# A decoder layer on one core: the second slice of the experts' down product as three split products, and the halves of the up split exchanged between VectorE and GpSimd

## The chip, the core and the metric

The kernel runs on one core of a Trainium2 chip. The metric is the device time of one execution in microseconds (us). The kernel before the change took 1047.9 us (median of three runs, 1045.63 to 1049.46).

## What is computed

One decoder layer for 896 tokens (8 sequences of 112) of width 512, all in float32: self-attention with 16 heads and a window mask, cross-attention with 16 heads of 128 over 375 context rows, and a feed-forward layer of one shared expert (hidden width 704, which the kernel takes as two units of 352) and 8 routed experts (hidden width 352), two of them per token. A layer norm follows each. The change touches only the routed experts:

```python
for e in range(N_EXPERTS):
    we = jnp.sum(jnp.where(topk_idx == e, w, 0.0), axis=-1)
    gu = xf @ up_w[e].T
    g_e, u_e = jnp.split(gu, 2, axis=-1)
    h = jax.nn.silu(g_e) * u_e
    out = out + h @ down_w[e].T * we[:, None]
```

## The kernel before

**Precision.** TensorE's products are taken in one of two ways. Most go through `three_products` (L84 to L88): both operands are split into a high part in the type fp32r and a low part, the rest, and high x high, low x high and high x low are added in one PSUM bank. A few are plain float32 matmuls. Making a split costs a cast on ScalarE (high) and a subtraction on VectorE or GpSimd (low = raw - high).

**Sorted blocks.** The tokens' rows are scattered to a buffer in HBM (`sorted_x`), sorted by expert, in NB = 21 blocks of 128 rows; each block belongs to one expert and has its own load of that expert's weights. Unit u = j + 1 serves block j; unit 22 (LAST_U) is the second half of the shared expert. A unit is 4 chunks of up weights (each 128 x 704) and 3 slices of down weights (each 128 x 512; the third has 96 rows that count). The raw weights and the low up parts lie in rings of three buffers (`raw`, `low`), the high up parts in two (`high`).

**One block step j**, the unit in which this text counts:

- TensorE (L2305 to L2313): `block_up(j)` (24 matmuls of 352 columns), `turn_block(j + 1)` (4 transposes, the next block's rows), `block_down(j - 1)`, `turn_hidden(j)` (3 transposes of the hidden block). `block_up` waits for the split rows `xb_lo` and both halves of its unit's low up parts; `turn_hidden` waits for `mul_done`, the hidden block.
- ScalarE (L1535 to L1543): `up_high(j + 2)` casts four chunks, then silu, `block_x(j + 1)` (high part of the next rows), `hidden_out(j)` (copies the turned hidden block out of PSUM), `third_high(j)` (cast of the third down slice).
- VectorE (L1895 to L1908): `up_low(j + 2)` subtracts chunks 0 and 1, then the product that makes `h_blk` (L1899, sets `mul_done`), `block_low(j + 1)` (`xb_lo`), `take(j - 1)` (a down result out of PSUM), `hidden_third_low(j)`, `third_low(j)`.
- GpSimd (L1320 to L1326): chunks 2 and 3 of the same `up_low`, and nothing else in this stage.
- The SP queue starts the loads and stores of every block.

All these are instruction streams written out by hand; each engine runs its own in order, and semaphores join them. The order on an engine is thus the order of the lines. `block_down` before the change (L2204 to L2217) takes slices 1 and 2 of the hidden width as float32 matmuls on `hT` and the raw weights, and slice 3 by `three_products`:

```python
for c in range(2):
    w = slice(DC * CHUNK + c * D, DC * CHUNK + (c + 1) * D)
    pe.matmul(ey_ps[:, n % 2, :], hT[:, c * P:(c + 1) * P], raw[u % RING][:, w], start=(c == 0), stop=False)
```

**After the blocks** comes the last unit: six steps k of `dense_up`, whose VectorE part (L1910 to L1918) also adds the gathered expert rows to the result (`combine`, three per step) and splits the last down weights (`down_low`, at k == 4), then the down products and the last layer norm.

Of the kernel before, what the change touches and what calls it, by code (L numbers as in the profile page):

```python
# [185 lines left out]
def expert_views(nc):  # L186

    F, E, NB = F32, EXPERTS, SLOT_TILES
    pad = 2 * 2 * TOK + 2 * HT + 2 * 2 * KVP + 2 * KT_N * PW - 2 * HC * TOK - 4 * HT
    front = [("h_hi", [HC, TOK], F32R), ("h_lo", [HC, TOK], F32R), ("silu_g", [2, HT], F), ("h_full", [2, HT], F), ("pad", [pad], F),  # L190
             ("y_sb", [2, D], F), ("gate_w", [DC, E], F), ("gate_b", [E], F), ("gate_hl", [DC, 2, E], F32R),
             ("before", [P], F32R), ("every", [P], F32R), ("iota_e", [TILES, E], F), ("level", [E, TILES], F), ("upto", [E, E], F),
             ("iota_j", [NB, E], F)]
    blocks = [("x_nat", [2, D], F), ("xb_hi", [D], F32R), ("xb_lo", [D], F32R),
              ("h_blk", [HPAD], F), ("hT", [2 * P], F), ("h3_hi", [P], F32R), ("h3_lo", [P], F32R), ("logitsT", [TOK], F), ("score", [TILES, E], F), ("chosen", [TILES, E], F),
              ("onehot", [2, TILES, E], F), ("weighed", [2, TILES, E], F), ("picked", [TILES, E], F32R), ("slot_of", [TILES, E], F),
              ("top_v", [TILES, 8], F), ("top_i", [TILES, 8], U32), ("top_f", [TILES, 8], F), ("top_w", [2, TILES], F),
              ("total", [2, TILES], F), ("mix", [2, TILES], F), ("over", [E, TILES], F), ("run", [E, E], F), ("n_tiles", [E], F),
              ("ends", [E], F), ("starts", [E], F), ("passed", [NB, E], F), ("owner_f", [NB], F), ("owner", [NB], U32),
              ("slots_f", [2 * TILES], F), ("slots", [2 * TILES], U32)]  # L200
# [734 lines left out]
def cross_and_experts(nc, env, w_pairs, ctx_nat, ctx_split, gateT, gate_bias, w_units, sorted_x, sorted_y, out, ended):  # L935
# [11 lines left out]
    with ExitStack() as es:  # L947
# [3 lines left out]
        def ps(name, shape):  # L951
# [15 lines left out]
        n_tiles, ends, starts, passed = v["n_tiles"], v["ends"], v["starts"], v["passed"]  # L967
        owner_f, owner, slots_f, slots = v["owner_f"], v["owner"], v["slots_f"], v["slots"]
        gu_ps, et_ps, ey_ps = v["gu_ps"], v["et_ps"], v["ey_ps"]
        h3_hi, h3_lo = v["h3_hi"], v["h3_lo"]  # L970
        THIRD = slice(UNIT_W - D, UNIT_W)
        rest = HID - 2 * P
        first_down_ps = [ey_ps[:, 0], ey_ps[:, 1], gu_ps[:, 0, 0], gu_ps[:, 0, 1], gu_ps[:, 1, 0], gu_ps[:, 1, 1], ey_ps[:, 0]]

# [35 lines left out]
        names_x = """gate_loaded consts_set more_consts gate_hi_done gate_lo_done logitsT_ready logitsT_copied logits_ready logits_added  # L1010
            logits_exp router places_ready owner_ready slots_ready cleared xb_turned xb_hi_done xb_lo_done
            up_ready silu_done mul_done h_hi_done h_lo_done h_turned
            hT_done h3_hi_done h3_lo_done third_hi_done third_lo_done y_ready y_taken y_stored combined stored""".split()
        names_x += [f"{part}_{k}_loaded" for part in ("up", "down") for k in range(1, RING)]
        names_x += [f"x_{k}_loaded" for k in range(2)] + [f"y_{k}_stored" for k in range(2)]
        names_x += [f"scattered_{t}" for t in range(TILES)]
# [217 lines left out]
        def _(pool):  # L1234
# [84 lines left out]

            def up_low(u):  # L1320

                for c in (2, 3):
                    cols = slice(c * CHUNK, (c + 1) * CHUNK)
                    pool.wait_ge(xs["up_hi_done"], DC * u + c + 1)
                    pool.tensor_tensor(low[u % RING][:, cols], raw[u % RING][:, cols], high[u % 2][:, c, :].bitcast(F32),
                                       ALU.subtract).then_inc(xs["up_lo_g"], 1)  # L1326
# [38 lines left out]
        def _(act):  # L1365
# [96 lines left out]
            def third_high(j):  # L1462
# [3 lines left out]
                act.wait_ge(xs["y_ready"], TILES + max(j - 1, 0))  # L1466
                act.copy(down_hi[0:rest, j % 2 * D:(j % 2 + 1) * D], raw[u % RING][0:rest, THIRD]).then_inc(xs["third_hi_done"], 1)

            def hidden_out(j):

                act.wait_ge(xs["h_turned"], j + 1)
                act.copy(hT[:], et_ps[:, 1, 0:2 * P]).then_inc(xs["hT_done"], 1)
                act.copy(h3_hi[0:rest], et_ps[0:rest, 1, 2 * P:3 * P]).then_inc(xs["h3_hi_done"], 1)

            def block_x(j):
                act.wait_ge(xs["xb_turned"], j + 1)
# [76 lines left out]
        def _(dve):  # L1553
# [232 lines left out]
            def third_low(j):  # L1786
# [4 lines left out]
                dve.tensor_tensor(down_lo[0:rest, j % 2 * D:(j % 2 + 1) * D], raw[u % RING][0:rest, THIRD], part.bitcast(F32),  # L1791
                                  ALU.subtract).then_inc(xs["third_lo_done"], 1)

            def hidden_third_low(j):

                dve.wait_ge(xs["h3_hi_done"], j + 1)
                dve.tensor_tensor(h3_lo[0:rest], et_ps[0:rest, 1, 2 * P:3 * P], h3_hi[0:rest].bitcast(F32),
                                  ALU.subtract).then_inc(xs["h3_lo_done"], 1)

            def combine(n):  # L1800

# [87 lines left out]
            for t in range(TILES - 1):  # L1889
                add_shared(t, 0)  # L1890
                if t in (2, 4):
                    up_low(1, t // 2 - 1)
                if t == TILES - 3:
                    block_low(0)
            for j in range(NB):  # L1895
# [10 lines left out]
                    take(j - 1)  # L1906
                hidden_third_low(j)
                third_low(j)  # L1908
            take(NB - 1)
            gated(0, UPS + NB)  # L1910
            for k in range(1, UPS):
                gated(k, UPS + NB)
                hidden_low(1, k - 1)
                if k == 4:
                    down_low(1, LAST_U)
                for n in range(3 * k - 3, min(3 * k, GATHERS)):
                    combine(n)
# [10 lines left out]
        def _(pe):  # L1928
# [265 lines left out]
            def turn_hidden(j):  # L2194

                pe.wait_ge(xs["mul_done"], UPS + j + 1)
                if j >= 1:
                    pe.wait_ge(xs["hT_done"], j)
                    pe.wait_ge(xs["h3_lo_done"], j)
                for c in range(HC):  # L2200
                    mm = pe.transpose(et_ps[:, 1, c * P:(c + 1) * P], h_blk[:, c * P:(c + 1) * P], ident[:])
                mm.then_inc(xs["h_turned"], 1)
# [1 line left out]
            def block_down(j):  # L2204
# [2 lines left out]
                pe.wait_ge(xs["hT_done"], j + 1)  # L2207
                pe.wait_ge(xs[f"down_{u % RING}_loaded"], 16 * (u // RING + 1))
                pe.wait_ge(xs["y_taken"], n - 1)
                for c in range(2):  # L2210
                    w = slice(DC * CHUNK + c * D, DC * CHUNK + (c + 1) * D)
                    pe.matmul(ey_ps[:, n % 2, :], hT[:, c * P:(c + 1) * P], raw[u % RING][:, w], start=(c == 0), stop=False)  # L2212
                pe.wait_ge(xs["h3_lo_done"], j + 1)
                pe.wait_ge(xs["third_lo_done"], j + 1)
                third = slice(j % 2 * D, (j % 2 + 1) * D)
                three_products(pe, ey_ps[:, n % 2, :], h3_hi[0:rest], h3_lo[0:rest], down_hi[0:rest, third], down_lo[0:rest, third],
                               False, True).then_inc(xs["y_ready"], 1)  # L2217

            def output(t, bank):

# [194 lines left out]
```

## Time and profile before

| what | value |
|---|---|
| three runs, median | 1047.9 us (1045.63, 1047.9, 1049.46) |
| the profiled execution, its own time | 1046.03 us |
| its span, first to last instruction | 1044.3 us |
| granted TensorE clock, mean | 0.999 of full speed |
| busy share of the span: TensorE / VectorE / ScalarE / GpSimd | 98% / 69% / 51% / 51% |
| the block stage | about 844 to 991 us, 21 steps of some 7.0 us |
| the last unit and the end | about 991 to 1044 us |

The busy share of an engine is the part of the span in which one of its instructions was being worked on. It is a mean over stages with different limits, so the text below reads the block stage by itself. The three runs differ by 0.37%.

### The profile page before, as it was taken

To read this page: it belongs to the slowest core of one execution; us is meant where nothing else is said; L and a number is where in the kernel's file an instruction comes from. 1 tells how busy PE (TensorE), PEld (TensorE's weight loads), DVE (VectorE), ACT (ScalarE), POOL (GpSimd) and SP (SyncE) were. 2 spreads that over 40 slices of the span, in tenths; PEclk is the share of its full clock that TensorE was granted. 3 is DMA by queue.
4 is the path that set the end of the run, shared out by engine and by line. 5 is a ranking of instruction groups with operands and counts; after the bars stand their busy time and mean duration, and the time that the engine had idled before them with its cause. 6 is when DMAs were issued, how large, how long until landed. Compare 5 with 4: busy or idle time off the path is not lost.

```text
span 1044.3 us, 20310 instructions
## 1 busy us (share of the span) xinstructions
PE 1018.9 (98%) x7021; PEld 910.0 (87%) x7021; DVE 722.6 (69%) x1496; ACT 536.6 (51%) x1075; POOL 532.7 (51%) x515
## 2 busy tenths in 40 slices
PE   8999999999999999999999999999999999999997
PEld 8856678999999999999999999999987888888885
DVE  4268876776767767767776776766886476666648
ACT  5355555555545455455555554554553356676610
POOL 1257767745534634643634634634474545544544
PEclk9999999999999999999999999999999999999999
DMA  8100114324333233323223233234220779999843
GB/s 279 83 32 2 61 39 153 143 109 157 116 108 114 99 107 111 101 109 116 96 111 115 94 117 109 98 118 136 98 90 1 286 282 386 387 393 399 294 119 113
DMA packets 45273, 153.46 MB, mean 147 GB/s; under 512 B 3768, under 2 KB 4792, under 8 KB 42144
## 3 DMA queue, kind: packets, MB, share of 16 engines
q1 hardware_dynamic: 42976, 145.38, 38.6%
q0 software_dynamic: 2240, 7.34, 2.1%
q8 instruction: 34, 0.56, 0.2%
q14 instruction: 23, 0.19, 0.0%
HBM read 130.04 MB, written 22.66 MB: 146 GB/s over the span
## 4 chain that ended last, share of the span: by engine, by line
PE 72%; POOL 5%; DVE 4%; issue 3%; ACT 1%; DMA 1%; POOLq 0%; DVEq 0%; ACTq 0%
PE xa_y_ps L86 6%; PE xa_y_ps L88 5%; PE xa_y_ps L87 5%; PE ex_raw_gu_ps L86 4%; PE ex_raw_gu_ps L88 4%; PE ex_raw_gu_ps L87 4%; PE xa_c_ps L1990 4%; PE xa_c_ps L1986 4%; PE xa_c_ps L1985 3%; PE ex_raw_ey_ps L2212 3%; PE xa_turn_ps L2067 3%; PE xa_turn_ps L2023 3%; PE front_k_ps L86 3%; PE front_k_ps L88 3%; PE front_k_ps L87 3%
## 5 line engine op out<-in xcount | busy, mean ns | idle before, releaser
L1300 POOL TENSOR_TENSOR xa_probs<-xa_probs,xa_inv_sum 112x750 f32<-112x750 f32 x63 | 97.9, 1553 | 75.5 <-DVE xa_inv_sum L1640 75.5
L1589 DVE TENSOR_TENSOR xa_kT_lo<-xa_turn_ps,xa_kT_hi 128x750 fp32r<-128x750 f32 x63 | 59.2, 939 | 99.9 <-ACT xa_kT_hi L1388 99.8
L1285 POOL TENSOR_TENSOR k_ms<-k_ss,sum_eps 125x6 f32<-125x6 f32 x63 | 12.6, 200 | 210.8 <-DVE k_ss L1605 210.8
L1985 PE MATMUL xa_c_ps<-xa_probsT_hi,xa_nat 125*128 125x224 f32 x384 | 92.3, 274 | 2.7 <-ACT xa_probsT_hi L1404 2.7
L1986 PE MATMUL xa_c_ps<-xa_probsT_hi,xa_nat 125*128 125x224 f32 x384 | 92.3, 275 | 0.0
L1404 ACT CAST xa_probsT_hi<-xa_turn_ps 125x672 fp32r<-125x672 f32 x62 | 44.6, 720 | 87.2 <-PE xa_turn_ps L2067 87.2
L1288 POOL TENSOR_TENSOR k_inv<-k_ms,neg_half 125x6 f32<-125x6 f32 x63 | 83.5, 1325 | 8.3 <-POOL k_ms L1285 6.7
L1410 ACT ACTIVATE xa_probs<-xa_scores_ps,xa_bias,xa_q_scale 112x375 f32<-112x375 f32 x126 | 82.8, 663 | 5.9 <-DVE xa_bias L1615 4.7
L1985 PEld LDWEIGHTS xa_c_ps<-xa_probsT_hi,xa_nat 125*128 125x128 f32 x384 | 73.6, 192 | 3.5 <-issue 3.1
L1986 PEld LDWEIGHTS xa_c_ps<-xa_probsT_hi,xa_nat 125*128 125x128 f32 x384 | 73.5, 191 | 0.5
L86 PE MATMUL front_k_ps<-land_xa_wk_hi,land_xa_ctx 128*125 128x256 f32 x252 | 71.4, 283 | 1.6 <-DVE front_k_hat L1632 1.2
L87 PE MATMUL front_k_ps<-land_xa_wk_hi,land_xa_ctx 128*125 128x256 f32 x252 | 70.8, 281 | 0.0
L88 PE MATMUL front_k_ps<-land_xa_wk_lo,land_xa_ctx 128*125 128x256 f32 x252 | 70.8, 281 | 0.0
L1384 ACT ACTIVATE front_k_sq<-front_k_ps 125x512 f32<-125x512 f32 x63 | 37.7, 598 | 62.0 <-PE front_k_ps L88 60.4
L1990 PE MATMUL xa_c_ps<-xa_probsT_lo,xa_nat 125*128 125x224 f32 x384 | 64.0, 275 | 0.8 <-DVE xa_probsT_lo L1621 0.8
L1584 DVE TENSOR_TENSOR xa_cT_lo<-xa_c_ps,xa_cT_hi 128x448 fp32r<-128x448 f32 x61 | 38.0, 622 | 37.9 <-ACT xa_cT_hi L1379 37.9
L1605 DVE TENSOR_REDUCE k_ss<-front_k_sq 125x6 f32<-125x768 f32 x63 | 59.7, 948 | 5.7 <-ACT front_k_sq L1392 5.7
L423 POOL TENSOR_TENSOR sa_masked<-sa_masked,sa_row_max 112x448 f32<-112x448 f32 x32 | 30.3, 947 | 60.5 <-DVE sa_row_max L653 60.0
L1392 ACT ACTIVATE front_k_sq<-xa_k_ps 125x256 f32<-125x256 f32 x63 | 24.3, 386 | 70.7 <-PE xa_k_ps L88 70.7
L1379 ACT CAST xa_cT_hi<-xa_c_ps 128x448 fp32r<-128x448 f32 x61 | 32.6, 535 | 52.4 <-PE xa_c_ps L1990 52.4
L1611 DVE TENSOR_REDUCE xa_row_max<-xa_scores_ps 112x2 f32<-112x750 f32 x63 | 58.4, 928 | 0.0
L1621 DVE TENSOR_TENSOR xa_probsT_lo<-xa_turn_ps,xa_probsT_hi 125x672 fp32r<-125x672 f32 x62 | 53.1, 856 | 5.3 <-ACT xa_probsT_hi L1404 4.7
(423 smaller groups left out, 3545.0 us busy)
## 6 DMA issues: line engine op xcount, KB each, us to landing
xa_nat<-ctx_split SPq DMA_DIRECT2D x56, 750.0 KB
ex_raw_raw<-in_w_units SPq DMA_DIRECT2D x15, 1408.0 KB, 8.2
ex_raw_raw<-in_w_units SPq DMA_DIRECT2D x15, 768.0 KB
land_ex_raw<-in_w_units SPq DMA_DIRECT2D x8, 1408.0 KB, 8.3
land_ex_raw<-in_w_units SPq DMA_DIRECT2D x8, 768.0 KB, 8.0
ctx_split<-xa_nat SPq DMA_DIRECT2D x8, 750.0 KB
sorted_x<-ex_raw_y_sb SPq DMA_DIRECT2D x7, 768.0 KB, 10.6
ex_raw_x_nat<-sorted_x SPq DMA_DIRECT2D x21, 256.0 KB, 8.6
```

The lines of the kernel that those rows point to most:

```text
L86: pe.matmul(out, st_hi, mv_hi, start=first, stop=False)
L87: pe.matmul(out, st_lo, mv_hi, start=False, stop=False)
L88: return pe.matmul(out, st_hi, mv_lo, start=False, stop=last)
L1288: pool.tensor_tensor(k_inv[0:KT, :], k_ms[0:KT, :], env["neg_half"][0:KT, 0:2 * KT_N], ALU.pow).then_inc(sem["kinv_done"], 1)
L1300: pool.tensor_tensor(probs[0:T, u % 2], probs[0:T, u % 2], inv_sum[0:T, u % 2, :].unsqueeze(2).broadcast_to([T, 2, KV]), ALU.mult).then_in ...
L1410: act.activation(probs[0:T, u % 2, h, :], scores_ps[0:T, h, 0:KV], ACT.Exp, bias=bias[0:T, u % 2, h:h + 1], scale=q_scale[0:T, u % B // HA ...
L1589: dve.tensor_tensor(kT_lo[:, :, 0:KV], turn_ps[:, :, 0:KV], kT_hi[:, :, 0:KV].bitcast(F32), ALU.subtract).then_inc(sem["kT_lo_done"], 1)
L1605: dve.tensor_reduce(k_ss[0:KT, :], k_sq[0:KT, :].rearrange("p (a d) -> p a d", d=XA_DH), AX_X, ALU.add).then_inc(sem["kss_done"], 1)
L1611: dve.tensor_reduce(row_max[0:T, u % 2, :], scores_ps[0:T, :, 0:KV], AX_X, ALU.max).then_inc(sem["max_done"], 1)
L1985: pe.matmul(c_view[:, c], nat[0:KT, u % 2, 0, at], probsT_hi[0:KT, :, cols], start=(t == 0), stop=False)
L1986: pe.matmul(c_view[:, c], nat[0:KT, u % 2, 1, at], probsT_hi[0:KT, :, cols], start=False, stop=False)
L1990: mm = pe.matmul(c_view[:, c], nat[0:KT, u % 2, 0, at], probsT_lo[0:KT, :, cols], start=False, stop=(t == KT_N - 1))
```

## The change

Three edits. (1) In `block_down` the second slice of the hidden width goes through `three_products`, after the third; for it ScalarE casts 256 columns of the turned hidden block to fp32r, copies 128 and casts a second down slice (`second_high`), and VectorE subtracts 256 columns and that slice (`second_low`). (2) In `up_low` GpSimd now takes chunks 0 and 1 and VectorE chunks 2 and 3; this holds for units 1 to 22 (unit 0 is split elsewhere). (3) In the last unit `down_low` moves from k == 4 to k == 3.

```diff
@@ gpsimd, up_low @@
-    for c in (2, 3):
+    for c in (0, 1):
@@ scalar @@
+def second_high(j):
+    u = j + 1
+    act.wait_ge(xs["y_ready"], TILES + j)
+    act.copy(second_hi, raw[u % RING][:, SECOND]).then_inc(xs["second_hi_done"], 1)
...
 def hidden_out(j):
     act.wait_ge(xs["h_turned"], j + 1)
-    act.copy(hT[:], et_ps[:, 1, 0:2 * P]).then_inc(xs["hT_done"], 1)
-    act.copy(h3_hi[0:rest], et_ps[0:rest, 1, 2 * P:3 * P]).then_inc(xs["h3_hi_done"], 1)
+    act.copy(h23_hi[:], et_ps[:, 1, P:3 * P]).then_inc(xs["h23_hi_done"], 1)
+    act.copy(hT[:], et_ps[:, 1, 0:P]).then_inc(xs["hT_done"], 1)
...
     hidden_out(j)
     third_high(j)
+    second_high(j)
@@ vector, up_low @@
-    for c in chunks or (0, 1):
+    for c in chunks or (2, 3):
...
+def second_low(j):
+    u = j + 1
+    dve.wait_ge(xs["second_hi_done"], j + 1)
+    dve.tensor_tensor(second_lo, raw[u % RING][:, SECOND], second_hi.bitcast(F32),
+                      ALU.subtract).then_inc(xs["second_lo_done"], 1)
...
 def hidden_third_low(j):
-    dve.wait_ge(xs["h3_hi_done"], j + 1)
-    dve.tensor_tensor(h3_lo[0:rest], et_ps[0:rest, 1, 2 * P:3 * P], h3_hi[0:rest].bitcast(F32),
-                      ALU.subtract).then_inc(xs["h3_lo_done"], 1)
+    dve.wait_ge(xs["hT_done"], j + 1)
+    dve.tensor_tensor(h23_lo[:], et_ps[:, 1, P:3 * P], h23_hi[:].bitcast(F32),
+                      ALU.subtract).then_inc(xs["h23_lo_done"], 1)
...
     hidden_third_low(j)
     third_low(j)
+    second_low(j)
...
-    if k == 4:
+    if k == 3:
         down_low(1, LAST_U)
@@ tensor, block_down @@
-    for c in range(2):
-        w = slice(DC * CHUNK + c * D, DC * CHUNK + (c + 1) * D)
-        pe.matmul(ey_ps[:, n % 2, :], hT[:, c * P:(c + 1) * P], raw[u % RING][:, w], start=(c == 0), stop=False)
-    pe.wait_ge(xs["h3_lo_done"], j + 1)
+    bank = ey_ps[:, n % 2, :]
+    pe.matmul(bank, hT[:], raw[u % RING][:, DC * CHUNK:DC * CHUNK + D], start=True, stop=False)
+    pe.wait_ge(xs["h23_lo_done"], j + 1)
     pe.wait_ge(xs["third_lo_done"], j + 1)
     third = slice(j % 2 * D, (j % 2 + 1) * D)
-    three_products(pe, ey_ps[:, n % 2, :], h3_hi[0:rest], h3_lo[0:rest], down_hi[0:rest, third], down_lo[0:rest, third],
-                   False, True).then_inc(xs["y_ready"], 1)
+    three_products(pe, bank, h23_hi[0:rest, P:2 * P], h23_lo[0:rest, P:2 * P], down_hi[0:rest, third], down_lo[0:rest, third],
+                   False, False)
+    pe.wait_ge(xs["second_lo_done"], j + 1)
+    three_products(pe, bank, h23_hi[:, 0:P], h23_lo[:, 0:P], second_hi, second_lo, False, True).then_inc(xs["y_ready"], 1)
```

What stands in a row on the engines that matter. In these rows the lines of the changed kernel are its own, and the tile names are those of the buffers as the program first gave them (`ex_raw_h_hi` is `h3_hi` or `h23_hi`, `land_ex_down_hi` holds the high down slices, `ex_low_low` and `land_low_low` are buffers of `low`).

VectorE, one block step, before:

```order
L1791 TENSOR_TENSOR land_ex_down_lo<-ex_raw_raw,land_ex_down_hi 96x512
L1667 TENSOR_TENSOR ex_low_low<-ex_raw_raw,land_ex_up_hi 128x704 x2
L1899 TENSOR_TENSOR ex_raw_h_blk<-ex_raw_silu_g,ex_raw_gu_ps 128x352
L1675 TENSOR_TENSOR ex_raw_xb_lo<-ex_raw_et_ps,ex_raw_xb_hi 128x512
L1784 COPY ex_raw_y_sb<-ex_raw_ey_ps 128x512
L1797 TENSOR_TENSOR ex_raw_h_lo<-ex_raw_et_ps,ex_raw_h_hi 96x128
```

and the same step after the change:

```order
L1799 TENSOR_TENSOR land_ex_down_lo<-ex_raw_raw,land_ex_down_hi 96x512
L1806 TENSOR_TENSOR land_ex_down_lo<-ex_raw_raw,land_ex_down_hi 128x512
L1675 TENSOR_TENSOR ex_low_low<-ex_raw_raw,land_ex_up_hi 128x704 x2
L1914 TENSOR_TENSOR ex_raw_h_blk<-ex_raw_silu_g,ex_raw_gu_ps 128x352
L1683 TENSOR_TENSOR ex_raw_xb_lo<-ex_raw_et_ps,ex_raw_xb_hi 128x512
L1792 COPY ex_raw_y_sb<-ex_raw_ey_ps 128x512
L1812 TENSOR_TENSOR ex_raw_h_lo<-ex_raw_et_ps,ex_raw_h_hi 128x256
```

One subtraction (L1806) is new, one is wider (L1812), and the pair of low up parts, still ahead of the product that makes `h_blk`, is now that of chunks 2 and 3.

ScalarE, one block step after the change; before, L1474 was not there, the first cast had 96 x 128 and the copy, ahead of it, 128 x 256:

```order
L1479 CAST ex_raw_h_hi<-ex_raw_et_ps 128x256
L1480 COPY ex_raw_hT<-ex_raw_et_ps 128x128
L1468 CAST land_ex_down_hi<-ex_raw_raw 96x512
L1474 CAST land_ex_down_hi<-ex_raw_raw 128x512
L1437 CAST land_ex_up_hi<-ex_raw_raw 128x704 x4
L1546 ACTIVATE ex_raw_silu_g<-ex_raw_gu_ps 128x352
L1486 CAST ex_raw_xb_hi<-ex_raw_et_ps 128x512
```

The four casts of the up chunks and everything behind them stand one 128 x 512 cast later.

## Rows read from the trace of the kernel before

**Rows 1.** Windows of two block steps: busy us of each engine, clock, DMA share
```profile
core 0: us, PE busy (x) PEld busy (x) DVE busy (x) ACT busy (x) POOL busy (x), PEclk, DMA share, GB/s
893.80:900.80 7.00, 7.00 (x39) 5.82 (x38) 4.55 (x8) 4.78 (x10) 3.48 (x2) 1.00 1.02 386
900.80:907.80 7.00, 7.00 (x40) 5.85 (x39) 4.51 (x8) 4.75 (x10) 3.48 (x2) 1.00 1.01 405
```
**Rows 2.** Chain that ended last, one block step: start us, us, what
```profile
899.98 0.21 PE ex_raw_gu_ps L86
...
903.86 0.44 PE ex_raw_et_ps L2173 x4
904.29 1.72 PE ex_raw_ey_ps L2212 x4
906.01 0.23 PE ex_raw_ey_ps L86
906.24 0.23 PE ex_raw_ey_ps L87
906.47 0.23 PE ex_raw_ey_ps L88
906.70 0.33 PE ex_raw_et_ps L2201 x3
907.03 0.18 PE ex_raw_gu_ps L86
```
**Rows 3.** Timeline of ScalarE, the same step: start us, us, instruction [idle before]
```profile
900.02 0.37 ACT L1472 COPY ex_raw_hT<-ex_raw_et_ps 128x256 f32<-128x256 f32 x1 [2.17 <-PE ex_raw_et_ps L2201]
900.29 0.26 ACT L1473 CAST ex_raw_h_hi<-ex_raw_et_ps 96x128 fp32r<-96x128 f32 x1
900.45 0.62 ACT L1467 CAST land_ex_down_hi<-ex_raw_raw 96x512 fp32r<-96x512 f32 x1
900.97 2.83 ACT L1436 CAST land_ex_up_hi<-ex_raw_raw 128x704 fp32r<-128x704 f32 x4
903.89 0.46 ACT L1539 ACTIVATE ex_raw_silu_g<-ex_raw_gu_ps 128x352 f32<-128x352 f32 x1
904.33 0.59 ACT L1479 CAST ex_raw_xb_hi<-ex_raw_et_ps 128x512 fp32r<-128x512 f32 x1
```
**Rows 4.** Timeline of VectorE, the same step
```profile
901.10 0.69 DVE L1791 TENSOR_TENSOR land_ex_down_lo<-ex_raw_raw,land_ex_down_hi 96x512 fp32r<-96x512 f32 x1 [0.23 <-ACT land_ex_down_hi L1467]
901.78 1.69 DVE L1667 TENSOR_TENSOR ex_low_low<-ex_raw_raw,land_ex_up_hi 128x704 fp32r<-128x704 f32 x2
904.39 0.52 DVE L1899 TENSOR_TENSOR ex_raw_h_blk<-ex_raw_silu_g,ex_raw_gu_ps 128x352 f32<-128x352 f32 x1 [0.91 <-ACT ex_raw_silu_g L1539]
904.95 0.69 DVE L1675 TENSOR_TENSOR ex_raw_xb_lo<-ex_raw_et_ps,ex_raw_xb_hi 128x512 fp32r<-128x512 f32 x1
```
**Rows 5.** Timeline of GpSimd, the same step
```profile
903.19 3.48 POOL L1325 TENSOR_TENSOR ex_low_low<-ex_raw_raw,land_ex_up_hi 128x704 fp32r<-128x704 f32 x2 [3.54 <-ACT land_ex_up_hi L1436]
```
**Rows 6.** Timeline of VectorE and GpSimd in the first block step
```profile
844.45 0.88 DVE L1667 TENSOR_TENSOR ex_low_low<-ex_raw_raw,land_ex_up_hi 128x704 fp32r<-128x704 f32 x1
845.25 2.40 DVE L1667 TENSOR_TENSOR ex_low_low<-ex_raw_raw,land_ex_up_hi 128x704 fp32r<-128x704 f32 x1
844.45 2.45 POOL L1325 TENSOR_TENSOR ex_low_low<-ex_raw_raw,land_ex_up_hi 128x704 fp32r<-128x704 f32 x1 [4.92 <-ACT land_ex_up_hi L1436]
846.86 2.36 POOL L1325 TENSOR_TENSOR ex_low_low<-ex_raw_raw,land_ex_up_hi 128x704 fp32r<-128x704 f32 x1
```
**Rows 7.** Timeline of VectorE and GpSimd in the cross-attention
```profile
666.05 1.44 POOL L1300 TENSOR_TENSOR xa_probs<-xa_probs,xa_inv_sum 112x750 f32<-112x750 f32 x1 [1.44 <-DVE xa_inv_sum L1640]
667.45 1.18 POOL L1242 TENSOR_TENSOR xa_q_ms<-xa_q_ss,sum_eps 112x4 f32<-112x4 f32 x1
666.41 2.16 DVE L1053 TENSOR_TENSOR xa_wo_lo<-xa_wo_raw,xa_wo_hi 128x1024 fp32r<-128x1024 f32 x1
```
**Rows 8.** Line L1053: count, duration ns min/median/max, first and last start
```profile
L1053 DVE TENSOR_TENSOR xa_wo_lo<-xa_wo_raw,xa_wo_hi x8: 1330/2159/2165, 188.5 to 746.0; 128x1024 fp32r<-128x1024 f32 x8
```
**Rows 9.** Line L1899, the same columns
```profile
L1899 DVE TENSOR_TENSOR ex_raw_h_blk<-ex_raw_silu_g,ex_raw_gu_ps x21: 520/521/522, 848.4 to 988.9; 128x352 f32<-128x352 f32 x21
```
**Rows 10.** Timeline of VectorE in the last unit
```profile
1015.08 1.63 DVE L1807 SCALAR_TENSOR_TENSOR resid<-ex_raw_raw,ex_raw_mix,resid 128x512 f32<-128x512 f32 x2
1017.08 0.76 DVE L1807 SCALAR_TENSOR_TENSOR resid<-ex_raw_raw,ex_raw_mix,resid 128x512 f32<-128x512 f32 x1 [0.37 <-DMA ex_raw_raw<-sorted_y,ex_raw_slots]
1018.90 0.62 DVE L1753 TENSOR_TENSOR ex_raw_h_full<-ex_raw_silu_g,ex_raw_gu_ps 128x448 f32<-128x448 f32 x1 [1.07 <-issue]
1020.04 1.75 DVE L1679 TENSOR_TENSOR land_ex_down_lo<-ex_raw_raw,land_ex_down_hi 128x1536 fp32r<-128x1536 f32 x1
```

More of the change, by code:

```diff
@@ L194, in expert_views @@
     blocks = [("x_nat", [2, D], F), ("xb_hi", [D], F32R), ("xb_lo", [D], F32R),
-              ("h_blk", [HPAD], F), ("hT", [2 * P], F), ("h3_hi", [P], F32R), ("h3_lo", [P], F32R), ("logitsT", [TOK], F), ("score", [TILES, E], F), ("chosen", [TILES, E], F),
+              ("h_blk", [HPAD], F), ("hT", [P], F), ("h23_hi", [2 * P], F32R), ("h23_lo", [2 * P], F32R), ("logitsT", [TOK], F), ("score", [TILES, E], F), ("chosen", [TILES, E], F),
               ("onehot", [2, TILES, E], F), ("weighed", [2, TILES, E], F), ("picked", [TILES, E], F32R), ("slot_of", [TILES, E], F),
@@ L969, in cross_and_experts @@
         gu_ps, et_ps, ey_ps = v["gu_ps"], v["et_ps"], v["ey_ps"]
-        h3_hi, h3_lo = v["h3_hi"], v["h3_lo"]
-        THIRD = slice(UNIT_W - D, UNIT_W)
+        h23_hi, h23_lo = v["h23_hi"], v["h23_lo"]
+        SECOND, THIRD = slice(UNIT_W - 2 * D, UNIT_W - D), slice(UNIT_W - D, UNIT_W)
+        second_hi, second_lo = down_hi[:, 2 * D:3 * D], down_lo[:, 2 * D:3 * D]
         rest = HID - 2 * P
@@ L1012, in cross_and_experts @@
             up_ready silu_done mul_done h_hi_done h_lo_done h_turned
-            hT_done h3_hi_done h3_lo_done third_hi_done third_lo_done y_ready y_taken y_stored combined stored""".split()
+            hT_done h23_hi_done h23_lo_done second_hi_done second_lo_done third_hi_done third_lo_done y_ready y_taken y_stored combined stored""".split()
         names_x += [f"{part}_{k}_loaded" for part in ("up", "down") for k in range(1, RING)]
@@ L1891, in _ @@
                 if t in (2, 4):
-                    up_low(1, t // 2 - 1)
+                    up_low(1, t // 2 + 1)
                 if t == TILES - 3:
@@ L2198, in turn_hidden @@
                     pe.wait_ge(xs["hT_done"], j)
-                    pe.wait_ge(xs["h3_lo_done"], j)
+                    pe.wait_ge(xs["h23_lo_done"], j)
                 for c in range(HC):
```

## The prediction

> **What bounds the kernel now.** I read the table of busy shares first and then only the block stage, where all but one small edit lies. The windows of two block steps [rows 1] show TensorE busy for 7.00 of 7.00 us at a clock of 1.00, ScalarE 4.8, VectorE 4.5, GpSimd 3.5. The chain of waits [rows 2] runs through TensorE alone: 24 up matmuls from 899.98, four transposes at 903.86, two float32 down products (four pieces, 1.72), three split products of 0.23, three transposes, and the next step at 907.03. So a step is 7.05 us of TensorE work. DMA is full as well (share 1.01 to 1.02, 386 to 405 GB/s), yet nothing on TensorE waits for it.
>
> The other engines are to be read by when they end. I count from H, the end of `turn_hidden(j)` (899.98 in the rows). ScalarE starts at H+0.04, its four up casts begin at H+0.99 and end at H+3.82, and silu starts at H+3.91, 0.03 after TensorE's last up matmul [rows 3]: no slack ahead of silu. VectorE makes its two low up parts from H+1.80 to 3.49 and then waits for silu [rows 4]. GpSimd starts on its parts at H+3.21 and ends at H+6.69 [rows 5], 0.36 before TensorE wants them. Thus VectorE's pair and GpSimd's pair hardly overlap in time.
>
> **Part 1: the product itself.** Removed per block: one float32 product, 1.72/2 = 0.86. Added: three at 0.23 = 0.70 [rows 2]. TensorE's work falls by 0.16, to 6.89 a step; over 21 blocks 3.4 us, if TensorE stays the bound.
>
> The Trainium skill (FP8 and Floating Point Precision, TensorE Precision Notes) says that a true float32 product makes four passes through the array. Three passes against four would save a quarter of 0.86, 0.215 a block and 4.5 us in all, as an estimate. The rows have 0.23 for each split product rather than 0.215, and I go by the rows.
>
> **Part 2: ScalarE.** The cast of 256 columns and the copy of 128 have the column counts of the two rows before, in the other order, and cost the same 0.43 until the next start. New is `second_high`, 512 columns: from the third slice's cast to the next start is 0.52 [rows 3]. Its own start waits for nothing new: the down product that frees its buffer ends before H. So the up casts start at H+1.51, 0.52 later. Each takes 0.68 to the next and 0.78 in all ((2.83-0.78)/3), so they end at H+2.29, 2.97, 3.66, 4.34. Silu starts at about 4.27 and ends at 4.73, 0.36 later than before. TensorE wants the hidden block at 6.56 (4.31, the end of the transposes, plus 0.86 + 1.40 for the down product, with 0.01 of rounding): alone, this is hidden.
>
> **Part 3: VectorE and GpSimd.** `hidden_third_low` grows from 128 to 256 columns, by some 0.13; it ends before `third_low` can start, at H+1.13. `second_low` adds one 0.69 subtraction, from about 1.81 to 2.50. GpSimd now may start once the first up cast is done, at 2.29 + 0.08 = 2.37. VectorE's pair needs the third and the fourth cast and can't start before 3.70. So the exchange, which starts GpSimd earlier, puts the two pairs on top of each other.
>
> What that costs is in two other stages. In the first block step both engines started a low part at 844.45 [rows 6]. VectorE's first took its usual 0.88; GpSimd's took 2.45 instead of some 1.7; VectorE's second took 2.40 instead of 0.88; GpSimd's second 2.36. In the cross-attention [rows 7] VectorE issued a 1024-column subtraction of two SBUF operands at 666.41 while GpSimd's multiply ran to 667.49. It took 2.16, against 1.33 for the shortest of the eight [rows 8], and ended 1.08 after that multiply: beside it, it can't have done more than a small part of its work. GpSimd's next instruction, on four columns, then took 1.18. One engine stands still until the other's whole instruction is done. The product that makes `h_blk`, with one operand in PSUM, took 520 to 522 ns in all 21 steps [rows 9], though in steps like this one GpSimd was at work beside it [rows 5].
>
> The Trainium skill (SBUF — State Buffer, Who interferes with whom) states the same as a rule against this change: a VectorE instruction with two SBUF inputs and a GpSimd instruction that reads SBUF hold a shared port in turn, each for its whole length. The traces agree.
>
> Now one step. A GpSimd part holds the port for some 1.6 and a VectorE part for 0.75 (846.86 to 847.65 in [rows 6], less the wait). GpSimd's first part asks at 2.37, waits for `second_low` until about 2.47 and ends at 4.1. VectorE's chunk 2, asking since 3.70, runs to 4.85. GpSimd's second part, asking since 4.1, runs to 6.45. VectorE's chunk 3 runs to 7.2. The turns alternate, as in [rows 6]. Queued behind chunk 3 on VectorE is the product for `h_blk`: 7.2 + 0.52 = 7.72. TensorE's `turn_hidden` waits for it until 7.78, where it was free at 6.56, and ends at 8.11. `xb_lo` follows at 7.71 to 8.40, so the next `block_up` starts 0.34 after the new H; the next step absorbs this, since its down product ends at H+6.9, ahead of 7.78. A step is thus 8.11 instead of 7.05: +1.06.
>
> It holds in steps 1 to 20. In step 0 the pairs collide before the change too [rows 6], silu ends later than they do, and no `second_high` stands ahead, so nothing changes there: 20 x 1.06 = 21.2 us.
>
> The bounds: if GpSimd keeps the port for both its parts, VectorE ends at about 7.4 and a step is 8.3 (+25 us). If GpSimd's first part doesn't lose 0.1 to `second_low`, a step is 8.0 (+19).
>
> **Part 4: `down_low` a step sooner.** It takes 1.75 and now runs at about 1015.1 to 1016.8, ahead of three `combine` steps, which end by about 1019.1 instead of 1017.8. VectorE was idle for 1.07 before 1018.9 [rows 10], so this fills the gap and at most 0.2 moves on. At its old place 1.75 fall away, behind which VectorE soon waits for silu again. I take 0; it may give 0.1.
>
> **Sum**, against the profiled execution's own 1046.0: +21.2 in the blocks, -0.2 for the last block's down product, which is on TensorE's path, 0 at the end: **1067 us**. The median of the runs is 1.9 above the profiled one; I leave the number and let the range carry it.
>
> **The rivals.** (A) *VectorE gets the port for both its chunks in a row, before GpSimd's second part.* This is the case on the other side. Its place is 4.85 in the step: if chunk 3, ready since 4.34, goes next, VectorE ends at 5.6 and `h_blk` at 6.2, before TensorE wants it. GpSimd then ends at 7.2, and `block_up` waits 0.35 in every second step: a mean of 7.07, 1046 us, no change. It decides at the point where VectorE's pair ends before about 6.0. Against it: in [rows 6] GpSimd cut in after one VectorE part. Chance 0.08. (B) *No blocking in this stage.* Then the pairs end at 5.3 and 5.7, all hidden, and Part 1 comes through: 1042.6, if DMA, already full [rows 1], can give 2% more. Against it stand [rows 6 to 8]. Chance 0.06. (C) *The two engines share instead of taking turns.* In [rows 6] VectorE did 1.69 of work in 3.20. At that rate, from 3.70 on, its pair ends at 6.9 and a step is 7.8: +15, 1061 us. For it: the sums in [rows 6] fit as well. Against it: the times in [rows 7]. Chance 0.13. (D) *Worse still*: TensorE, idle for 1.2 of 8.1 us, is granted less clock, or blocks lose more than I count. The clock reads 1.00 in both windows, but they have no idle time. Above 1075 us, chance 0.03.
>
> **Numbers.** Main case 0.70. The range holds the main case with its bounds (1065 to 1071), up to 2 us for the median's distance, and most of C: 1056 to 1074. A change of 0.5% (5.2 us) is about what can be told from none. Slower: main, C and D, 0.86. Same: A and nearly all of B (3.4 us is 0.33%), 0.12. Faster, which asks for half as much again as B gives: 0.02.
>
> **What would show it.** Right: windows of block steps with TensorE idle for some 1.1 us in each, that idle put down to VectorE's `h_blk`; block steps 8.1 long; low parts on VectorE recorded at well over 0.88 (2.0 and more for chunk 3), on GpSimd over 1.7; DMA share near 0.87. Wrong: VectorE's low parts at 0.88 in all steps (then B), both ending by H+5.7 with GpSimd's second part over 3 us long (then A), or a wait that ends with a cast of ScalarE or a DMA.

## The result and the profile after

The changed kernel takes **1072.27 us** (median of four runs, 1068.14 to 1072.81), the kernel before 1048.08 (four runs, 1045.63 to 1049.46): a ratio of 1.0223, interval 1.0195 to 1.0250. The forecast was 1067, range 1056 to 1074, slower with a chance of 0.86. The profiled execution took 1068.14 (span 1066.4, mean clock 0.999), 22.1 above the profiled one of before; the sum had said 21.0.

The page's first part for the kernel after: busy time, share of the span, instructions.

```profile
PE 1023.4 (96%) x7042; PEld 912.0 (86%) x7042; DVE 768.3 (72%) x1517; ACT 545.3 (51%) x1096; POOL 543.4 (51%) x515
```

TensorE reads as 96% busy, which hides what happened. ScalarE reads the turned hidden block once per block, first by L1472 (a copy) before and by L1479 (a cast) after. Between the first and the last of these 21 instructions lay 140.5 us before, 7.03 a step, and 163.5 after, 8.18 a step. These 20 steps took 23.0 us more, and the rest of the program 0.9 less. Two block steps of after in windows, same columns as [rows 1]:

```profile
899.53:907.70 8.17, 7.30 (x39) 5.99 (x39) 6.80 (x9) 5.18 (x10) 4.02 (x2) 1.00 0.94 338
907.70:915.90 8.20, 7.30 (x39) 5.99 (x39) 6.83 (x9) 5.18 (x10) 4.02 (x2) 1.00 0.94 322
```

TensorE is busy for 7.30 of 8.17 and of 8.20 us where it had no idle time before. VectorE went from 4.5 to 6.8 busy and GpSimd from 3.48 to 4.02, though GpSimd still makes two subtractions of the same size. The clock stays at 1.00.

The chain of waits of after, one step (start us, us, what), to be held against [rows 2]:

```profile
908.79 0.52 ACT land_ex_down_hi L1474
909.31 2.05 ACT land_ex_up_hi L1437 x3
911.36 0.02 issue
911.38 1.60 DVE ex_low_low L1675 x2
912.99 1.77 issue
914.76 0.52 DVE ex_raw_h_blk L1914
915.28 0.04 issue
915.32 0.56 PE ex_raw_et_ps L2217 x3
```

Before, this chain ran through TensorE alone. Now it goes through ScalarE's casts, then `up_low`, then `h_blk`, and TensorE has only its three transposes on it. The 1.77 called "issue" is time in which VectorE stands inside its pair and no record says why.

The timelines of VectorE and of GpSimd in that step (start us, us, instruction, idle before), against [rows 4, 5]:

```profile
909.43 0.68 DVE L1806 TENSOR_TENSOR land_ex_down_lo<-ex_raw_raw,land_ex_down_hi 128x512 fp32r<-128x512 f32 x1
911.38 3.45 DVE L1675 TENSOR_TENSOR ex_low_low<-ex_raw_raw,land_ex_up_hi 128x704 fp32r<-128x704 f32 x2 [1.27 <-ACT land_ex_up_hi L1437]
914.76 0.51 DVE L1914 TENSOR_TENSOR ex_raw_h_blk<-ex_raw_silu_g,ex_raw_gu_ps 128x352 f32<-128x352 f32 x1
915.19 0.68 DVE L1683 TENSOR_TENSOR ex_raw_xb_lo<-ex_raw_et_ps,ex_raw_xb_hi 128x512 fp32r<-128x512 f32 x1
```

GpSimd in the same view:

```profile
910.07 4.02 POOL L1326 TENSOR_TENSOR ex_low_low<-ex_raw_raw,land_ex_up_hi 128x704 fp32r<-128x704 f32 x2 [4.15 <-ACT land_ex_up_hi L1437]
```

VectorE's pair takes 3.45 for what took 1.69, and GpSimd's, from 910.07 to 914.09, runs beside it for 2.7 us. The subtractions have the same 128 x 704 as before. In numbers from H = 907.71: GpSimd asks at 2.36 (forecast 2.37) and ends at 6.38 (6.45). VectorE's pair starts at 3.67 (3.70) and ends at 7.12 (7.2). TensorE's down product ends at 6.85 (6.9), and `turn_hidden` starts at 7.61 (7.78) and ends at 8.17 (8.11).

The waits on TensorE in the block stage of after (us in total, times, longest us):

```profile
PEld ex_raw_et_ps L2217 <- DVE ex_raw_h_blk L1914: 24.5, 20, 1.6
...
PE ex_raw_et_ps L2217 <- DVE ex_raw_h_blk L1914: 15.8, 20, 1.2
```

Twenty times, once for each step 1 to 20, the hidden block is late. No wait of this size on a cast or a DMA stands beside it.

### The profile page after: what moved, and what is told of

Read it like the earlier page. It is cut to its first block, busy times and chain, and to the rows that moved or that the text cites. A ratio compares the mean times of both kernels' runs of the same rounds, so it can differ in the third digit from the quotient of the medians.

```text
span 1066.4 us, 20394 instructions
## 1 busy us (share of the span) xinstructions
PE 1023.4 (96%) x7042; PEld 912.0 (86%) x7042; DVE 768.3 (72%) x1517; ACT 545.3 (51%) x1096; POOL 543.4 (51%) x515
## 4 chain that ended last, share of the span: by engine, by line
PE 60%; ACT 8%; DVE 7%; issue 6%; POOL 4%; POOLq 0%; ACTq 0%; DVEq 0%
PE xa_y_ps L86 6%; PE xa_y_ps L88 5%; PE xa_y_ps L87 5%; PE xa_c_ps L2006 4%; PE xa_c_ps L2002 3%; PE xa_c_ps L2001 3%; PE xa_turn_ps L2083 3%; PE xa_turn_ps L2039 3%; PE front_k_ps L86 3%; PE front_k_ps L88 3%; PE front_k_ps L87 3%; PE ex_raw_gu_ps L86 2%; PE ex_raw_gu_ps L87 2%; PE ex_raw_gu_ps L88 2%; PE xa_scores_ps L2069 2%
```

## The experiments

My theory: a VectorE subtraction with two SBUF operands and a GpSimd subtraction that reads SBUF use one port in turns, each for its whole length. The exchange puts the pairs on top of each other, and `h_blk`, queued behind VectorE's pair, carries the delay to TensorE. Rivals: ScalarE's new cast or VectorE's new subtraction is what makes `h_blk` late, with nothing to do with GpSimd; the two engines' writes collide as well as their reads; the second product itself costs more than it saves. Ratios are to the kernel before on the same chip with their 95% interval. "A step" is the stretch between the first and the last time that ScalarE first reads the turned hidden block, divided by 20, in the run's profile. In the edits, `...` stands for further lines of the same kind (names, and the counts that TensorE waits for).

**1. The change without the exchange.**

```diff
@@ GpSimd, up_low
-                for c in (0, 1):
+                for c in (2, 3):
@@ VectorE, up_low
-                for c in chunks or (2, 3):
+                for c in chunks or (0, 1):
@@ VectorE, the first unit's parts
-                    up_low(1, t // 2 + 1)
+                    up_low(1, t // 2 - 1)
```

> The changed kernel with the exchange alone undone: GpSimd again takes chunks 2 and 3, VectorE 0 and 1; the second product as three split products and the earlier down_low stay. Turn-taking at the port (my theory): VectorE's pair is over by H+3.9, GpSimd's runs from about H+3.9 to H+7.2, TensorE waits some 0.3 us for it in part of the steps: a step of 7.05 to 7.15 us, ratio to before 0.998 to 1.003. Rival, the added ScalarE cast and VectorE subtraction are what costs: all of them are still there, so the time stays near 1.02. Rival, sharing instead of turns: like my theory here, within 1.00.

Measured: 1049.40 us, ratio 1.0020 (1.0007 to 1.0033); a step 7.22, a little above the 7.05 to 7.15 expected. Nearly all of the loss is gone. ScalarE's extra cast and VectorE's extra subtraction are both still there, so neither makes it by itself. From the timelines of VectorE and GpSimd in this run:

```profile
910.66 1.69 DVE L1675 TENSOR_TENSOR ex_low_low<-ex_raw_raw,land_ex_up_lo 128x704 fp32r<-128x704 f32 x2
...
912.06 3.49 POOL L1326 TENSOR_TENSOR ex_low_low<-ex_raw_raw,land_ex_up_lo 128x704 fp32r<-128x704 f32 x2 [4.13 <-ACT land_ex_up_lo L1437]
```

Both pairs have their old lengths. But without the exchange the second product gives nothing either: the casts are later, so GpSimd's pair ends later, and `block_up` now waits for it in half the steps (waits of the block stage; us, times, longest):

```profile
PE ex_raw_gu_ps L86 <- POOL ex_low_low L1326: 3.1, 6, 0.5
...
PE ex_raw_gu_ps L86 <- POOL land_low_low L1326: 2.0, 4, 0.5
```

**2. The exchange alone, on the kernel before** (experiment 1's lines the other way round).

> The kernel before with the exchange alone: GpSimd chunks 0 and 1, VectorE 2 and 3; no second split product. Turn-taking: GpSimd asks at H+1.86, VectorE's first part at H+3.2, the four parts end at about H+6.6 on VectorE, the hidden block at H+7.1: a step of 7.6 to 7.8 us, +11 to +15 us, ratio 1.011 to 1.014. VectorE's parts are recorded at about 1.1 and 2.4 us. Sharing in proportion: VectorE's pair takes 3.2 from H+3.2, a step of about 7.35, ratio 1.006. Rival, the added work costs and not the exchange: ratio 1.000.

Measured: 1062.63 us, 1.0144 (1.0124 to 1.0165); a step 7.63, against 7.03 before and 8.18 after. VectorE's pair, in the timeline of this run, is as long as in the change:

```profile
913.64 3.45 DVE L1667 TENSOR_TENSOR ex_low_low<-ex_raw_raw,land_ex_up_hi 128x704 fp32r<-128x704 f32 x2 [1.36 <-ACT land_ex_up_hi L1436]
```

So the exchange is enough to lose. It loses 12.1 us in the 20 steps and not 23 because the casts come 0.52 earlier without `second_high`: 8.18 less 7.63 is 0.55. In the change, the new cast pushes an already late chain further; in experiment 1 the second product with the same cast costs 0.2 a step in all. The profiled execution of this run took 1067.79 us, the other four 1061.57 to 1063.32. The extra time of the profile lies outside the 20 steps, and most of it ahead of them: ScalarE's first read of the turned hidden block comes at 857.1, where it came at 850.7 before. The last section shows what stood in the way there.

**3. GpSimd's subtraction replaced by two memsets**, which write as many columns and read nothing. Left out: the low weights of chunks 0 and 1, which are zeros here.

```diff
-                    pool.tensor_tensor(low[u % RING][:, cols], raw[u % RING][:, cols], high[u % 2][:, c, :].bitcast(F32),
-                                       ALU.subtract).then_inc(xs["up_lo_g"], 1)
+                    pool.memset(low[u % RING][:, cols].bitcast(F32), 0.0).then_inc(xs["written"], 1)
+                    pool.wait_ge(xs["written"], 2 * (u - 1) + c + 1)
+                    pool.memset(low[u % RING][:, cols].bitcast(F32), 0.0).then_inc(xs["up_lo_g"], 1)
...
```

> The changed kernel, but GpSimd's two low parts are left out: in place of each subtraction it writes zeros over the same 704 columns twice, so it works beside VectorE's pair without reading SBUF. If what VectorE waits for is GpSimd's reading: VectorE's parts are back at 0.88 us each, the pair ends by H+5.3, a step is 6.85 to 6.95, ratio 0.995 to 1.000. If any GpSimd instruction that touches SBUF holds VectorE up: its parts are recorded at over 1 us, for each write of some 0.7 us one wait, the pair ends at H+6 or later, a step is 7.1 or more, ratio 1.00 to 1.01. If the added ScalarE and VectorE work is what costs: 1.02, as the changed kernel.

Measured: 1041.21 us, 0.9957 (0.9941 to 0.9972); a step 6.82, just below the 6.85 to 6.95 expected. The timelines of VectorE and GpSimd show them at work together with no delay:

```profile
908.65 1.69 DVE L1676 TENSOR_TENSOR ex_low_low<-ex_raw_raw,land_ex_up_lo 128x704 fp32r<-128x704 f32 x2 [1.27 <-ACT land_ex_up_lo L1438]
...
908.68 0.69 POOL L1326 MEMSET ex_low_low<- 128x704 f32 x1
909.42 0.69 POOL L1328 MEMSET ex_low_low<- 128x704 f32 x1
```

It isn't GpSimd's being at work, nor its writes; it is its reading beside VectorE's two SBUF operands. The Trainium skill (SBUF — State Buffer, Who interferes with whom) states that a VectorE instruction with two SBUF inputs contends with a GpSimd instruction that reads SBUF, and not with one that only writes it. This run agrees: 1.69 for VectorE's pair beside the memsets, as in experiment 1. That the port is taken for a whole instruction isn't tested here; experiment 7 shows it. The step of 6.82 is also what TensorE needs with the second product split and nothing in its way.

**4. All four low parts on VectorE.**

```diff
@@ GpSimd, up_low
-                for c in (0, 1):
+                for c in ():
@@ VectorE, up_low
-                for c in chunks or (2, 3):
+                for c in chunks or (0, 1, 2, 3):
@@ VectorE, the first unit's parts
-                    up_low(1, t // 2 + 1)
+                    up_low(1, *((0,) if t == 2 else (1, 2, 3)))
...
```

> The changed kernel with all four low parts on VectorE, none on GpSimd. Turn-taking: no one to wait for at the port; four parts back to back from H+2.35 to H+5.55, the hidden block at H+6.0, xb_lo at H+6.6, a step of 6.9 to 7.0, ratio 0.996 to 1.000. So twice the work on VectorE is over sooner than half of it beside GpSimd. Rival, VectorE's load or its place in the chain is what costs: 1.03 or more. Sharing: as turn-taking.

Measured: 1044.49 us, 0.9970 (0.9960 to 0.9980); a step 6.92. VectorE's timeline:

```profile
910.29 3.29 DVE L1675 TENSOR_TENSOR ex_low_low<-ex_raw_raw,land_ex_up_lo 128x704 fp32r<-128x704 f32 x4
```

Four parts in 3.29, where two beside GpSimd took 3.45. In the change, GpSimd's help cost VectorE more than doing the work itself. This also ends the rival that VectorE has too much to do.

**5. The last part behind the hidden block.** VectorE makes chunk 2 where it did, and chunk 3 only after `h_blk` and `xb_lo`. The pairs overlap as before; only what queues behind them changes.

```diff
-                up_low(j + 2)
+                up_low(j + 2, 2)
@@ after block_low(j + 1)
+                up_low(j + 2, 3)
```

> The changed kernel with one line moved on VectorE: chunk 3's low part goes behind the hidden block and xb_lo, chunk 2 stays ahead of them. The port sees the same four parts in the same turns, but the hidden block no longer queues behind the last. Turn-taking with the queue behind it as the price: the hidden block at H+5.3, TensorE's turn_hidden waits for nothing, chunk 3 ends at about H+7.2, which block_up of the next step waits for by 0.3 us in part of the steps: a step of 7.05 to 7.2, ratio 0.999 to 1.004. If the port's turns cost by themselves, wherever they stand in the queue: 1.02 as before the move.

Measured: 1049.77 us, 1.0039 (1.0024 to 1.0054); a step 7.23, just above the 7.05 to 7.2 expected. GpSimd's pair still takes 4.03, but VectorE's two parts are 1.17 and 0.94 (timeline of VectorE):

```profile
904.70 1.17 DVE L1675 TENSOR_TENSOR ex_low_low<-ex_raw_raw,land_ex_up_hi 128x704 fp32r<-128x704 f32 x1 [1.27 <-ACT land_ex_up_hi L1437]
906.06 0.52 DVE L1914 TENSOR_TENSOR ex_raw_h_blk<-ex_raw_silu_g,ex_raw_gu_ps 128x352 f32<-128x352 f32 x1 [0.19 <-ACT ex_raw_silu_g L1546]
...
907.22 0.94 DVE L1675 TENSOR_TENSOR ex_low_low<-ex_raw_raw,land_ex_up_hi 128x704 fp32r<-128x704 f32 x1
```

`h_blk`, which has an operand in PSUM, takes its usual 0.52 while GpSimd's pair (903.39 to 907.42) is under way, and the loss falls from 24 us (2.2%) to 4 (0.4%). What is left of it shows in the waits of the block stage: `block_up` waits for chunk 3's low part 10 times, for up to 0.5 us and 4.6 in all. What cost the time is not the turn itself but who stands behind it in VectorE's queue.

**6. Three parts on VectorE, the last one on GpSimd.** If the theory holds, the product's gain can be had: VectorE takes the chunks as they come, GpSimd only chunk 3, whose read falls at the end of VectorE's three.

```diff
@@ GpSimd, up_low
-                for c in (0, 1):
+                for c in (3,):
@@ VectorE, up_low
-                for c in chunks or (2, 3):
+                for c in chunks or (0, 1, 2):
@@ VectorE, the first unit's parts
-                    up_low(1, t // 2 + 1)
+                    up_low(1, *((0,) if t == 2 else (1, 2)))
@@ TensorE, the counts it waits for
-                pe.wait_ge(xs["up_lo_v"], 2 * (u + 1))
-                pe.wait_ge(xs["up_lo_g"], 2 * (u + 1))
+                pe.wait_ge(xs["up_lo_v"], 2 + 3 * u)
+                pe.wait_ge(xs["up_lo_g"], 2 + 1 * u)
...
```

> The changed kernel with the four low parts split 3 to 1: VectorE chunks 0, 1 and 2, GpSimd chunk 3. Turn-taking: a part holds the port 0.75 us on VectorE and 1.6 on GpSimd, so this frees 0.85 us of port time and puts the slow part last, where nothing queues behind it on VectorE. VectorE's three parts end at H+4.75, GpSimd's at H+6.35, the hidden block at H+5.2; TensorE never waits, a step is 6.89, ratio 0.996 to 0.998 (some 3.4 us less than before). Rival, VectorE's load is what costs: one more 0.8 us instruction per step makes it worse than the changed kernel, ratio 1.03 or more. Rival, DMA is the floor once TensorE has less to do: ratio 1.000.

Measured: 1042.01 us, 0.9948 (0.9931 to 0.9965), and in a second set of runs 1041.69, 0.9961 (0.9947 to 0.9975); a step 6.82. It beats both kernels: by the ratios some 29 us under the change and 5.5 under the kernel before, in the second set 4.1. The first ratio is below the 0.996 to 0.998 expected. The windows of two of its steps, same columns as [rows 1]:

```profile
893.80:900.60 6.80, 6.80 (x41) 6.00 (x40) 5.85 (x10) 5.09 (x11) 1.98 (x1) 1.00 1.02 419
900.60:907.50 6.90, 6.90 (x41) 6.09 (x40) 5.93 (x10) 5.17 (x11) 1.98 (x1) 1.00 1.01 401
```

TensorE has no idle time again, and its chain of waits runs through it alone, with the shape that the split product gives it:

```profile
909.31 0.44 PE ex_raw_et_ps L2189 x4
909.75 0.86 PE ex_raw_ey_ps L2227 x2
910.61 0.23 PE ex_raw_ey_ps L86
...
911.76 0.23 PE ex_raw_ey_ps L88
911.99 0.33 PE ex_raw_et_ps L2217 x3
```

The timelines of VectorE and GpSimd show where they meet:

```profile
907.82 2.48 DVE L1675 TENSOR_TENSOR ex_low_low<-ex_raw_raw,land_ex_up_lo 128x704 fp32r<-128x704 f32 x3
910.23 0.51 DVE L1914 TENSOR_TENSOR ex_raw_h_blk<-ex_raw_silu_g,ex_raw_gu_ps 128x352 f32<-128x352 f32 x1
...
909.90 1.98 POOL L1326 TENSOR_TENSOR ex_low_low<-ex_raw_raw,land_ex_up_lo 128x704 fp32r<-128x704 f32 x1 [4.87 <-ACT land_ex_up_lo L1437]
```

GpSimd asks at 909.90, is held for some 0.3 (1.98 against 1.7) until VectorE's third part is done at 910.30, and then reads beside `h_blk`, which takes its usual 0.51.

**7. The same 3 to 1 split, but GpSimd takes chunk 0** and VectorE chunks 1, 2 and 3. Shares of work as in experiment 6; only the place differs. The edit is that of experiment 6 with `(0,)` for GpSimd, `(1, 2, 3)` for VectorE and, for the first unit, `(1,)` and `(2, 3)`.

> The same 3 to 1 shares as the faster version, but GpSimd has chunk 0 and VectorE 1, 2 and 3. If place decides, and not the shares: GpSimd holds the port from H+2.4 to H+4.0, VectorE's first part waits for it from H+3.0 and its three end at H+6.4, the hidden block at H+6.9, turn_hidden late by some 0.4 us and slow to start: a step of 7.4 to 7.6, +7 to +11 us, ratio 1.007 to 1.010. If the smaller sum of port time is what made the 3 to 1 version fast: 0.995 to 0.998 again.

Measured: 1054.85 us, 1.0083 (1.0067 to 1.0098); a step 7.47. The timelines of VectorE and GpSimd:

```profile
906.96 3.44 DVE L1675 TENSOR_TENSOR ex_low_low<-ex_raw_raw,land_ex_up_hi 128x704 fp32r<-128x704 f32 x3 [0.59 <-ACT land_ex_up_hi L1437]
...
906.32 1.73 POOL L1326 TENSOR_TENSOR ex_low_low<-ex_raw_raw,land_ex_up_hi 128x704 fp32r<-128x704 f32 x1 [5.75 <-ACT land_ex_up_hi L1437]
```

One GpSimd part, which got the port first, costs VectorE about 1 us (3.44 against 2.48) and the kernel 13 us over experiment 6 (1041.69 on the same chip). So the place decides, not the share.

**8. The 3 to 1 split on the kernel before**, to see what of experiment 6's gain is the product's.

> The kernel before with the 3 to 1 split alone (VectorE chunks 0, 1, 2, GpSimd chunk 3), no second split product. The 3 to 1 version of the changed kernel was 0.9948. If its gain is the product's: TensorE has the same work as before, 7.0 a step, ratio 0.998 to 1.000; the little that may come is a wait for GpSimd's last part at the start of block_up. If the gain is the split's: 0.995.

Measured: 1045.67 us, 1.0001 (0.9992 to 1.0010); a step 7.00. The split of the parts alone gives nothing, since TensorE was the bound anyway. With the second product it is 6.82: 0.18 less a step, 3.8 us over 21 blocks. The medians on one chip say the same within their scatter: 1045.67 here, 1042.31 for experiment 6's kernel with the third edit undone.

**9. The third edit undone, on experiment 6's kernel**, taken twice. On the changed kernel itself it was not tried.

```diff
-                if k == 3:
+                if k == 4:
                     down_low(1, LAST_U)
```

> The 3 to 1 version with the third edit undone: down_low of the last unit back at k == 4. I counted that edit at 0, at most 0.1 us: the two versions within 0.1% of each other, ratio 0.994 to 0.996. If its earlier place is worth a wait of TensorE or of VectorE: 0.2% or more above the 3 to 1 version.

> The 3 to 1 version once more, beside the next one on the same chip: ratio 0.993 to 0.998.

> The 3 to 1 version with down_low back at k == 4, beside the one above on the same chip. Third edit worth nothing, my estimate: the medians within 1 us (0.1%). Worth a wait: 2 us or more apart.

Measured: `down_low` at its old place 1042.31 (0.9968, 0.9956 to 0.9980) and 1041.99 (0.9964, 0.9950 to 0.9977), at its new place 1042.01 and 1041.69. The second pair is the fair one, since both ran on one chip: 0.3 us in favour of the new place, inside the scatter of the runs (1041.64 to 1042.18 against 1041.79 to 1043.03). The first pair, on two chips, has the same distance, but its ratio of 0.9968 lies above the 0.994 to 0.996 expected. The step earlier is worth 0.3 us or nothing.

## Why the prediction was right

**What bounds the kernel**: right. A step of before was TensorE's, and experiments 6 and 8 show it again once nothing else is late.

**Part 1** (0.16 saved a step): right and a little low. Experiments 8 and 6 give 7.00 and 6.82, so 0.18. The rows of a single product gave 0.16. The Trainium skill (FP8 and Floating Point Precision, TensorE Precision Notes) gives a true float32 product four passes; three passes for four would save a quarter of 0.86, 0.215, as an estimate. The measured value lies between the two. In the change itself the saving is hidden behind the wait.

**Part 2** (ScalarE's 0.52): right in place. The up casts start 1.50 after H, as worked out at 1.51, and silu comes no later than VectorE can use it. What the prediction had not priced is what this 0.52 does without the exchange: in experiment 1 it pushes GpSimd's pair past the point where `block_up` wants it, and eats the product's gain.

**Part 3** (+1.06 a step): the mechanism held in every test. Its two halves are separate in experiments 1 (no overlap, 1.002), 3 (overlap without reads, 0.9957) and 5 (overlap, but nothing behind it, 1.0039). Measured step growth: 8.18 less 7.03 is 1.15. Against the worked-out times `h_blk` is ready about 0.2 sooner. Part of that is that it follows its predecessor by 0.07 before the recorded end, which I had not subtracted. In return the three transposes take 0.56, where I had put 0.33, which is what they add when TensorE comes to them straight from other work (the last section shows why). The two errors cancel to 0.06 (8.17 against 8.11). The rest of the difference is that a step of before was 7.03 on average and not 7.05, so 23.0 stands against 21.2: 1.8 us. The 0.34 by which `block_up` was to start late, and the next step to absorb, was right too: the down product was to end at H+6.9 and ends at 6.85, before `h_blk` is there. Two of the signs were off. TensorE's idle time is 0.87 to 0.90 a step and not 1.1, since the longer transposes count as busy, and the DMA share is 0.94 and not 0.87.

**Part 4** (0): right as far as experiment 9 shows it, on another kernel than the changed one.

**The rivals.** A (VectorE gets the port twice in a row) fell: its pair takes 3.45 in the steps looked at, and the single parts of the block stage run to 2.39. B (no blocking) fell by the result, and experiment 3 shows what it would have been: 0.43% under before, 4.5 us, where I had put 3.4. C (the engines share) would have given a pair until 6.9; it ended at 7.12 in the step shown. That alone is a small difference; in experiment 7, though, a GpSimd part with the port from 913.80 took 1.72, its undisturbed length, and VectorE's first part, issued at 914.44, took 1.83 and ended at 916.27, 0.75 after it: the whole delay on one side, which is a turn and not a share. D (less clock) fell: windows of after read 1.00 with 0.9 us idle in each step.

**The sum** was 1.1 us low against the profiled execution: 1.8 us too little in the blocks, less 0.7 that the rest of the program gave back beyond the 0.2 counted for the last block's down product. The 0.7 isn't explained. The median lies 4 us above the profiled execution, and the other three runs all lie there, with a mean clock of 0.997 to 0.998 against its 0.999. Why is open; the last section has a possible cause. The prediction allowed 2 us for this distance, and it was 4.1. So the median is 5.3 us above the forecast of 1067, and that it lies inside the range is partly luck: the room came from the bound of +25 us in the blocks, where GpSimd keeps the port for both its parts, and none of the steps looked at shows that.

## What to carry to other kernels

Before moving work between VectorE and GpSimd, mark in both timelines the instructions that read two SBUF operands on VectorE and those that read SBUF on GpSimd, and let them meet only where VectorE has nothing urgent queued behind. One GpSimd part in front of VectorE's chunks cost 13 us here over the same part behind them. `h_blk`, with one operand in PSUM, took 504 to 523 ns in all profiles. A split that starts the slower engine first looks balanced by busy time and puts the overlap where it hurts: read the ends, not the shares. And when two edits come together, price each with and without the other: here the second product with its later casts cost 3.8 us in the block steps without the exchange (144.3 against 140.5) and 10.9 with it (163.5 against 152.6).

## What the runs showed of the hardware that I had not expected

- **GpSimd keeps the port twice as long as VectorE** for the same 704 columns: some 1.6 against 0.75 us. In experiment 6 GpSimd's part ends 1.58 after VectorE's third (911.88, 910.30); in experiment 7 VectorE's first ends 0.75 after GpSimd's. So handing VectorE more work made it finish sooner (3.29 for four parts, 3.45 for two).
- **What three transposes add depends on what runs ahead of them.** They take 0.56 in the chain of after, behind a wait, and 0.33 in experiment 6, where TensorE never stops, at a granted clock of 1.00 in both. The single transposes are no slower: their records have a median of 273 ns after and 272 in experiment 6, and the last two start 0.11 apart in both. What differs is their first weight load (0.14). In experiment 6 it runs beside the product before, here it waits for `h_blk` and starts with the first transpose (timelines of TensorE's weight loads, experiment 6 and after):

```profile
911.61 0.48 PEld L2217 LDWEIGHTS ex_raw_et_ps<-ident,ex_raw_h_blk 128*128 128x128 f32 x3
...
915.32 0.31 PEld L2217 LDWEIGHTS ex_raw_et_ps<-ident,ex_raw_h_blk 128*128 128x128 f32 x3 [1.20 <-DVE ex_raw_h_blk L1914]
```

- **A tiny instruction can lose two turns.** In the profile of experiment 2, ahead of the block stage (timelines of VectorE and GpSimd):

```profile
837.43 4.02 DVE L1740 TENSOR_TENSOR ex_raw_total<-ex_raw_top_w 128x7 f32<-128x7 f32 x1
...
837.04 0.96 POOL L1349 DMA_INDIRECT sorted_x<-resid,ex_raw_slots  x1 [0.30 <-issue]
838.02 3.40 POOL L1325 TENSOR_TENSOR ex_low_low<-ex_raw_raw,land_ex_up_lo 128x704 fp32r<-128x704 f32 x2
```

A sum over seven columns, 0.17 us long in the twelve other profiles, stood until both GpSimd parts were over. It started while GpSimd was in an indirect DMA instruction, and so was there before either part began. Why it was held already then is open: in the profile of before the same sum took 0.17 beside such an instruction. So turns don't alternate always, which the prediction's bound (+25 us) had kept open. In this execution VectorE came late to `xb_lo`, TensorE stood idle for 2.7 us, from 845.84 to 848.56, and its windows (columns as in [rows 1]) show a lower clock there:

```profile
844.00:847.00 3.00, 1.84 (x9) 1.16 (x7) 3.00 (x5) 3.00 (x5) 1.85 (x2) 1.00 0.92 375
847.00:850.00 3.00, 1.44 (x5) 1.47 (x6) 3.00 (x5) 0.11 (x1) 2.13 (x1) 0.77 0.34 132
850.00:854.00 4.00, 4.00 (x21) 4.00 (x20) 0.68 (x1) 0.00 (x0) 0.00 (x0) 0.75 0.02 4
```

The clock falls from 1.00 to a mean of 0.77 and 0.75. In windows of 1 us it reads 1.00 up to 848, 0.81 in the next and 0.50, the lower of its two levels, from 849 to 852. In the profile of before the sum was over only 0.6 us ahead of GpSimd's first part. Whether the two meet in this place may be what lifts some executions of the same kernel by 3 to 4 us. Only this one profile shows a meeting, and no run was made to test it.
